# One VectorE scan instruction for two units in the first half of a selective scan

## The reference

```python
def step(h, inp):
    d_t, u_t, B_t, C_t = inp
    dA = jnp.exp(d_t[..., None] * A)
    dBu = (d_t * u_t)[..., None] * B_t[:, None, :]
    h = dA * h + dBu
    y = jnp.einsum('bdn,bn->bd', h, C_t)
    return (h, y)
```

## Time and profile before

| what | value |
|---|---|
| time, median of 3 runs | 2921.07 us |
| lowest and highest | 2912.21 and 2923.14 us |
| the profiled execution: its own time | 2925.61 us |
| its span in the trace | 2923.2 us |
| mean granted TensorE clock | 0.925 |
| exponentials of q = 0, first sequence | from 149.8 to 464.0 us |
| exponentials of q = 0, second sequence | from 894.2 to 1209.9 us |

### The profile page before, as it was taken

How to read it: one execution, slowest core, us unless ns; L and a number is a source line. 1 busy time by engine, 2 the same in 40 slices (tenths; PEclk the granted TensorE clock), 3 DMA queues, 4 the chain that set the end, 5 groups by cost and what they waited for, 6 DMA issues and landing times. The chain is left out here.

```text
span 2923.2 us, 38661 instructions
## 1 busy us (share of the span) xinstructions
PE 2360.5 (81%) x12388; PEld 1192.8 (41%) x12389; DVE 1950.6 (67%) x1758; ACT 1807.8 (62%) x2817; POOL 1311.9 (45%) x492
## 2 busy tenths in 40 slices
PE   5688888888887888888888766787778579969899
PEld 2244444444334444444444323223322345546444
DVE  4699999999768999999994565914841312225520
ACT  4799999999668999999983423064036311113331
POOL 2089998999706999899991111000000210020000
PEclk8899999999998999999998788798889789979999
DMA  2330001000114000100000210010001510020000
GB/s 79 90 80 25 29 25 40 28 26 25 49 53 110 29 25 26 39 29 25 29 15 17 80 68 1 1 35 26 1 20 36 223 35 22 22 82 1 9 1 29
DMA packets 60904, 115.70 MB, mean 40 GB/s; under 512 B 13683, under 2 KB 22003, under 8 KB 59648
## 3 DMA queue, kind: packets, MB, share of 16 engines
q1 hardware_dynamic: 52192, 103.26, 11.0%
q0 software_dynamic: 8608, 11.05, 1.3%
HBM read 86.46 MB, written 27.53 MB: 39 GB/s over the span
## 5 line engine op out<-in xcount | busy, mean ns | idle before, releaser
L926 POOL TENSOR_TENSOR hs<-hs,c_bc 128x2048 f32<-128x2048 f32 x256 | 1166.5, 4557 | 65.0 <-DVE hs L977 50.1
L977 DVE TENSOR_TENSOR_SCAN hs<-decays,carry,ps 128x512 f32<-128x512 f32 x512 | 621.7, 1271 | 10.1 <-PE ps L1004 9.3
L977 DVE TENSOR_TENSOR_SCAN hs<-decays,ps 128x512 f32<-128x512 f32 x512 | 611.0, 1216 | 24.9 <-PE ps L1004 6.7
L1012 PE MATMUL ps<-hs,sel 128*64 128x512 f32 x2048 | 499.8, 609 | 14.5 <-POOL hs L926 14.1
L1004 PE MATMUL ps<-ident,dbu_even 128*128 128x128 f32 x2048 | 295.1, 283 | 93.9 <-DVE hs L977 65.1
L1004 PE MATMUL ps<-ident,dbu_odd 128*128 128x128 f32 x2048 | 294.4, 283 | 91.8 <-DVE hs L977 60.5
L940 ACT ACTIVATE decays<-delta_far,A 128x512 f32<-128x512 f32 x512 | 355.5, 706 | 11.9 <-DVE hs L977 11.8
L940 ACT ACTIVATE decays<-delta_near,A 128x512 f32<-128x512 f32 x512 | 356.0, 706 | 2.0 <-DVE hs L977 1.9
L948 ACT ACTIVATE dbu_odd<-du_turned,b_turned 128x512 f32<-128x512 f32 x512 | 355.6, 706 | 0.0
L948 ACT ACTIVATE dbu_even<-du_turned,b_turned 128x512 f32<-128x512 f32 x496 | 344.4, 706 | 0.0
L1004 PEld LDWEIGHTS ps<-ident,dbu_even 128*128 128x128 f32 x2048 | 219.8, 141 | 244.1 <-DVE hs L977 194.2
(11 more groups left out here) (264 smaller groups left out, 2647.6 us busy)
## 6 DMA issues: line engine op xcount, KB each, us to landing
c_bc<-c_rows SPq DMA_DIRECT2D x256, 128.0 KB, 2.8
o_rows<-osb SPq DMA_DIRECT2D x32, 256.0 KB
u_rows<-u SPq DMA_DIRECT2D x4, 1024.0 KB, 4.5
d_rows<-delta SPq DMA_DIRECT2D x4, 1024.0 KB, 4.2
delta_near<-d_rows SPq DMA_DIRECT2D x4, 1024.0 KB, 9.8
hs<-u_rows SPq DMA_DIRECT2D x4, 1024.0 KB, 6.5
delta_far<-d_rows SPq DMA_DIRECT2D x4, 1024.0 KB, 11.9
w_down<-in_expert_proj SPq DMA_DIRECT2D x1, 4096.0 KB, 36.4
```

The costliest lines, as they stand in the source:

```text
L926: pool.tensor_tensor(x, x, spread(c_bc[:, g, :], 4), ALU.mult).then_inc(weighed.sem, 1)
L977: dve.tensor_tensor_scan(hs[:, quad % RING, n, :], decays[:, s % RING, :], ps[:, DBU + s % RING, :], carry[:, at(i * GB, g), blk] if q els ...
L1012: mm = pe.matmul(ps[lo:lo + DB, ACC + quad % 2 * 2 + j // 2, :], k.sel2[:, :], hs[:, quad % RING, j, :], start=False, stop=False, skip_gro ...
```

## The change

In the half q = 0, units are scanned two by two. DVE skips the even units and, at each odd one, issues one scan of 1024 columns over the two adjacent ring slots of decays, of PSUM banks and of the quad of states; it signals 2 at its end. Between the two units the first decay of the second is zero, so that the running state is dropped there: one memset at the start of each sequence's scan writes zeros into column 0 of all four ring slots, and in q = 0 the exponential of an odd unit writes only columns 1 to 511. With decay 0 at column 512 the second unit starts from its own increment, as it did with 0.0 as initial state. In q = 1 nothing is changed: units are scanned singly from `carry`, and the exponentials write all 512 columns.

```diff
--- before.py
+++ after.py
@@ -848,7 +848,7 @@
     decay, turned, scanned = k.sig("decay"), k.sig("dbu_turned"), k.sig("scanned")
     made = k.sig("dbu_made")
     weighed, summed, carried = k.sig("weighed"), k.sig("states_summed"), k.sig("carried")
-    skipped, gated = k.sig("skipped"), k.sig("gated")
+    skipped, gated, opened = k.sig("skipped"), k.sig("gated"), k.sig("decays_opened")
     u_here, far_here, again = k.sig("u_here"), k.sig("far_here"), k.sig("inputs_again")
     ACC, DBU = 0, 4
     U_SLOT = RING - 1
@@ -932,12 +932,16 @@
             act.sem_inc(made.sem, 1)
 
             def body(q, i):
+                first = isinstance(i, int) and i == 0
                 for s in range(UNITS):
                     g, blk = divmod(s, NB)
                     if q and isinstance(i, int) and (i, s) == (0, 0):
                         act.wait_ge(far_here.sem, far_here.at(16 * PAIR))
                     act.wait_ge(scanned.sem, count(scanned, q, i, UNITS, s + 1))
-                    act.activation(decays[:, s % RING, :], (far if q else near)[:, blk, :], ACT.Exp,
+                    if first and q == 0 and s == 0:
+                        act.wait_ge(opened.sem, opened.at(1))
+                    joined = 0 if q else s % 2
+                    act.activation(decays[:, s % RING, joined:W], (far if q else near)[:, blk, joined:W], ACT.Exp,
                                    scale=A[:, at(i * GB, g), blk]).then_inc(decay.sem, 1)
                     for place in range(MADE_AT[blk - 1] if blk else 0, MADE_AT[blk]):
                         n, t = divmod(place, QT)
@@ -951,6 +955,7 @@
 
         @block.vector
         def _(dve):
+            dve.memset(decays[:, :, 0:1], 0.0).then_inc(opened.sem, 1)
             dve.sem_inc(scanned.sem, RING)
 
             def gate(q):
@@ -972,11 +977,20 @@
                         dve.wait_ge(carried.sem, carried.at(LOOPS * QUADS - (2 if s == 0 else 0)))
                     if first and q and s == NB:
                         gate(q - 1)
+                    if q == 0 and s % 2 == 0:
+                        continue
                     dve.wait_ge(decay.sem, count(decay, q, i, UNITS, s + 1))
                     dve.wait_ge(turned.sem, count(turned, q, i, UNITS, 1 + s + 1))
-                    dve.tensor_tensor_scan(hs[:, quad % RING, n, :], decays[:, s % RING, :], ps[:, DBU + s % RING, :],
-                                           carry[:, at(i * GB, g), blk] if q else 0.0, ALU.mult, ALU.add)\
-                       .then_inc(scanned.sem, 1)
+                    if q:
+                        dve.tensor_tensor_scan(hs[:, quad % RING, n, :], decays[:, s % RING, :],
+                                               ps[:, DBU + s % RING, :], carry[:, at(i * GB, g), blk], ALU.mult,
+                                               ALU.add).then_inc(scanned.sem, 1)
+                    else:
+                        two = slice(s % RING - 1, s % RING + 1)
+                        dve.tensor_tensor_scan(hs[:, quad % RING, n - 1:n + 1, :].rearrange("p c n -> p (c n)"),
+                                               decays[:, two, :].rearrange("p c n -> p (c n)"),
+                                               ps[:, DBU + two.start:DBU + two.stop, :].rearrange("p c n -> p (c n)"),
+                                               0.0, ALU.mult, ALU.add).then_inc(scanned.sem, 2)
 
             all_bodies(dve, body)
             gate(CPB - 1)
@@ -1037,6 +1051,7 @@
     summed.passed(STATES * QUADS + RING)
     carried.passed(LOOPS * QUADS)
     skipped.passed(CPB)
+    opened.passed(1)
     gated.passed(CPB * CI)
     u_here.passed(16 * CPB)
     far_here.passed(16 * PAIR)
```

## The result

| | before | changed |
|---|---|---|
| time, median (5 runs each) | 2921.07 us | 2947.52 us |
| lowest to highest | 2912.21 to 2926.83 | 2939.41 to 2948.62 |
| ratio to before | | 1.0085, interval 1.0064 to 1.0106 |
| span of the profile | 2923.2 us | 2946.8 us |
| q = 0, first sequence | 314.2 | 325.6 |

A half q = 0 is counted from ACT's first exponential in it to its first in q = 1, a half q = 1 from there to the start of the gate products that end the scan. The four sum to 1283.4 us before and 1307.1 after, 23.7 more; the spans differ by 23.6. So the whole loss lies in the scan, and 22.6 of it in the two halves whose scans were joined. Outside the four halves the profiles of all kernels here have between 1631 and 1642 us, though nothing is changed there.

The account below looks back on a forecast made before the run. ACT was taken to set the pace in q = 0, DVE close behind. Terms of 5.5 + 4.5 + 1.5 - 0.2 us gave +11.3, so 2932.4 us from the median of 2921.07; range 2917 to 2946.

Parts of the forecast that it names:

- rival "faster": In q = 0 DVE is the pace after all, so all 38 us come back: 2883 us; chance 0.06.
- The saving: On DVE in q = 0, 0.15 us less for each of 256 pairs: 38 us, hidden beside ACT.
- rival "longer scan": The joined scan takes longer than 2.29 us; at 2.44 the time is 2942 us; chance 0.20.
- forecast "within 0.5%": The whole time changes by less than 14.6 us, forecast 0.39% more; chance 0.58.
- ACT loses 0.09 us a group: At block 0 in q = 0, ACT waits for the slot of blocks 4 and 5, 60 passages: 5.5 us.
- these three: Exponential to scan start 0.83 us, scan end to ACT 0.04, joined scan 2.29; error of each some 0.02.
- rival "no stall": Pair slots return 0.1 us sooner, the 5.5 us at block 0 vanish, some 6 remain: 2927 us; chance 0.19.
- The term of the start: Each sequence's start: late PE turns delay the scan of 12, 13 and ACT's 16th exponential, 2.4 and 2.1 us.
- The passages to q = 1: After q = 0's late last pair, the last quad's sums, load of u and skip product go 0.75 us later, twice: 1.5.

Follow-up runs that it names:

- e2: Kernel before with single scans, but in q = 0 DVE signals 2 after each odd unit and nothing after even ones; 2923.6 us, 1.0008 of before.

## Why the prediction was right and wrong

Right was what bounds the kernel. ACT sets the pace of q = 0, the joined scan takes 2.29 us, what it saves on DVE is worth nothing by itself, and the joined scan makes ACT wait at block 0 of each group and nowhere else in the steady part. The rival "faster" is out: q = 0 never fell below 313.9 us, whatever the scans, as long as ACT made all products. The saving was mis-sized, though, by a reading of durations where the spacing of starts counts: 38 us in the prediction, 12 by the spacing of scans that wait for nothing. It changed nothing in the sum, but the rival "faster" at 2883 promised three times what was there. The rival "longer scan" is out by the row at 2286 ns. Of the range 2917 to 2946 the median missed the upper end by 1.5 us (2921.07 times the ratio of 1.0085 is 2945.9, at the very edge), and the forecast "within 0.5%" was wrong: it is 0.85% slower, and the interval does not reach down to 0.5%. That interval is 0.2% to either side, so half a percent was also too much to call the least that a measurement of this kernel can tell.

The term that failed is the first, "ACT loses 0.09 us a group", 5.5 us in all. It measured 7.7 us in the first sequence (from the 16th exponential to q = 1: 301.96 us instead of 294.27) and 9.4 in the second (303.66 instead of 294.28), 17.1 together. The sum had been a small difference of large numbers, 3.16 - 3.07, so an error of 0.17 in two handovers tripled it:

- The 0.83 between an exponential's start and the scan's was read from a single scan. The joined scan of blocks 4 and 5 starts 0.89 to 0.90 behind, with 511 or 512 columns, and 0.96 inside the loop of the second sequence.
- The 0.04 from a scan's end to ACT's start was read at the end of q = 1, in a pass that stands outside the hardware loop. Outside the loop it is 0.04 for the joined scan too (the step of 0.78); inside, where 24 of the 30 counted passages of a sequence lie, it is 0.14, in both sequences. The row was right and stood for another place in the code.

I had called the error of these three "some 0.02" each, and used it only downwards, for the rival "no stall". It should have gone up as well: each 0.1 us there is 6 us in the time.

The term of the start, 2.4 + 2.1 us, measured 3.7 + 1.8. Its chain was right, but it took PE's lengths from rows and said nothing of the clock in which they were read. In the first sequence the two turns and the skip product fell into a granted clock of 0.50 and took 1.97 and 4.20 us instead of 1.09 and 3.60; in the second the skip product took 3.80 instead of the 4.79 of before. The one made the term larger, the other smaller, so that the sum of 5.5 us came near 4.5 by luck. That the pairs alone make most of it (run e2) I had not separated. The passages to q = 1 were put at 0.75 us each, and the links named there did move so: SP's load of u is issued 9.54 us after the half's first exponential instead of 8.92 and 8.93, and the skip product begins 14.98 and 14.92 after it instead of 14.31 and 14.30, 0.6 to 0.7 later. The whole halves q = 1 gave +3.2 in the first and -2.1 in the second sequence, 1.1 together, which is scatter and confirms nothing: in the seven profiled kernels with the same instructions in q = 1 these halves lie anywhere from 324.3 to 328.6 us. Sum of the measured terms: 17.1 + 5.5 + 1.1 = 23.7 us.

## What to carry to other kernels

Before an engine is made faster, look at starts, not at busy shares: here four evenly spaced starts with nothing to wait for between them told that ACT, and not DVE at 97%, was the pace, and that DVE's saving was worth nothing. Read the saving itself from starts too: two scans that wait for nothing stand 2.23 us apart from pair to pair where their durations add up to 2.44. Merging two instructions has a second price that the saved overhead hides: their buffers come back together and late, and on a ring of four slots that hits the tightest place in the producer's order; an order with even gaps, or more slots, removes it. When a forecast hangs on the difference of two near-equal times that is paid sixty times, take each handover from a row in the same loop and the same form of instruction, and carry its error into the range in both directions.

## What the runs showed of the hardware that I had not expected

A handover for which ACT waits costs 0.10 us more inside the hardware loop than in the same code written out (0.88 against 0.78 from start to start), and a register operation stands in it there; where ACT has not to wait, the loop costs nothing (0.613 a step in both). DVE shows something like it: a single scan starts 0.83 us behind its exponential inside the loop and 0.74 in the last pass, outside it. A joined scan of blocks 4 and 5 starts later, 0.89 or 0.96 inside and 0.90 outside. Scans overlap at their ends: of 1.22 us each they start 1.11 apart when nothing is waited for, and joined ones of 2.29 start 2.18 apart. And a DVE product that reads and writes SBUF waited for the end of POOL's multiplication, and POOL's copy for the end of the product, in both forms tried. This made a group of POOL's 9.7 us long with a tensor_scalar and 10.0 with a tensor_tensor, where two quads that wait for nothing would take 9.5 (twice 4.75).

The fastest kernels here are single scans with the skip product of q = 0 one quad earlier (2917.5 us, 0.9988 of before, 0.9978 to 0.9998) and joined scans with eight slots, that move and a tensor_scalar on DVE (2916.8, 0.9979, 0.9969 to 0.9989). Both beat the two kernels of this study; their intervals overlap, and nothing in them speaks for the joined scan.
